# Graph attention layer with residual norm: first row tile's score products as three matmuls of 512 columns, with the off-diagonal part copied and added

## The reference

```python
u = einsum('bld,bmd->blm', h, h) / sqrt(384)
delta = softmax(u) * adjacency
attn = delta / (sum(delta, axis=2) + 1e-10)
# attn is split into above the diagonal, diagonal and below it
ctx = attn_left @ (h @ W_left.T + b_left) + diag_a * (h @ W_self.T + b_self) + attn_right @ (h @ W_right.T + b_right)
out = layernorm(x + relu(layernorm(ctx) * gamma + beta))
```

## Time and profile before

| what | value |
|---|---|
| median of 3 runs | 460.52 us (460.16 to 460.91) |
| profiled execution, its own time | 460.05 us |
| its span, first to last instruction | 458.3 us |
| PE busy | 448.5 us (98%), 2639 matmuls |
| DVE busy | 386.4 us (84%) |
| ACT busy | 322.1 us (70%) |
| POOL busy | 208.7 us (46%) |
| granted TensorE clock, mean | 0.994 of full speed |

### The profile page before, as it was taken

The page is one execution under the profiler, slowest core; times in us unless marked ns, Lnnn a source line. Parts: engine busy times, 40 slices in busy tenths (PEclk is TensorE's granted clock), DMA queues, the critical chain, the costliest instruction groups (busy, mean ns, idle before and its releaser), DMA issues.

```text
span 458.3 us, 9720 instructions
## 1 busy us (share of the span) xinstructions
PE 448.5 (98%) x2639; PEld 446.4 (97%) x2639; DVE 386.4 (84%) x1366; ACT 322.1 (70%) x710; POOL 208.7 (46%) x293
## 2 busy tenths in 40 slices
PE   8999999999999999999999999999999999999993
PEld 8999999999999999999999999999999999999992
DVE  5877988888898888988888988888889888987876
ACT  6756677677678677677677778677677677777753
POOL 0144346553345553345543445553345553344542
PEclk9999999999999999999999999999999999999997
DMA  8765455666456665555666555666445565554222
GB/s 259 224 207 176 136 173 184 197 197 196 137 179 194 188 195 177 169 175 183 189 195 186 157 178 183 188 208 193 150 163 191 182 200 182 159 176 155 92 69 93
DMA packets 84135, 80.60 MB, mean 176 GB/s; under 512 B 7058, under 2 KB 76436, under 8 KB 84116
## 3 DMA queue, kind: packets, MB, share of 16 engines
q1 hardware_dynamic: 84112, 80.38, 55.4%
q10 hardware_dynamic: 4, 0.00, 0.0%
HBM read 52.04 MB, written 28.31 MB: 175 GB/s over the span
## 4 chain that ended last, share of the span: by engine, by line
issue 29%; POOL 22%; DVE 15%; ACT 11%; PE 9%; DMA 8%; SPq 6%; POOLq 0%; DVEq 0%; ACTq 0%
POOL scaled L1111 7%; DMA dt_raw<-dt_dram 6%; POOL shifted L1115 6%; ACT normed L640 4%; SPq L319 4%; POOL rstd L1105 4%; ACT ps_scores L594 3%; DVE y_sb L876 3%; DVE proj_lo L832 3%; PE ps_proj L497 3%; POOL dt_right L1099 3%; DVE delta L801 3%; DVE cross_turned L768 2%; POOL dt_left L1099 2%; ACT dt_full L624 2%
## 5 line engine op out<-in xcount | busy, mean ns | idle before, releaser
L497 PE MATMUL ps_proj<-w_hi,xt_split 128*128 128x384 f32 x1128 | 236.4, 334 | 0.5 <-ACT ps_proj L610 0.5
L497 PEld LDWEIGHTS ps_proj<-w_hi,xt_split 128*128 128x128 f32 x1128 | 199.1, 188 | 0.8 <-ACT ps_proj L610 0.8
L497 PE MATMUL ps_proj<-w_lo,xt_split 128*128 128x384 f32 x564 | 128.0, 334 | 0.0
L1105 POOL TENSOR_TENSOR rstd<-var_eps,minus_half 128x4 f32<-128x4 f32 x31 | 34.7, 1119 | 184.2 <-DVE var_eps L862 184.2
L497 PEld LDWEIGHTS ps_proj<-w_lo,xt_split 128*128 128x128 f32 x564 | 100.5, 188 | 0.0
L610 ACT ACTIVATE ps_proj<-bias 128x384 f32<-128x384 f32 x188 | 90.5, 494 | 1.4 <-DMA bias<-in_L_gnn_b_self 0.7
L1111 POOL TENSOR_TENSOR scaled<-normed,gamma_sb 128x384 f32<-128x384 f32 x60 | 61.7, 1028 | 31.9 <-ACT normed L640 31.9
L614 ACT ACTIVATE proj_hi<-ps_proj 128x384 fp32r<-128x384 f32 x128 | 63.4, 496 | 13.0 <-PE ps_proj L497 12.6
L634 ACT ACTIVATE ps_ctx<-ps_proj,diag 128x384 f32<-128x384 f32 x64 | 35.5, 555 | 49.4 <-PE ps_proj L497 49.3
L832 DVE TENSOR_TENSOR proj_lo<-ps_proj,proj_hi 128x384 fp32r<-128x384 f32 x128 | 67.3, 544 | 1.8 <-ACT proj_hi L614 1.6
L1115 POOL TENSOR_TENSOR shifted<-scaled,beta_sb 128x384 f32<-128x384 f32 x61 | 62.5, 1024 | 2.5
(11 more groups left out here) (104 smaller groups left out, 675.3 us busy)
## 6 DMA issues: line engine op xcount, KB each, us to landing
x_sb<-in_x SPq DMA_DIRECT2D x32, 384.0 KB, 4.5
xt_sb<-in_x_t SPq DMA_DIRECT2D x31, 384.0 KB, 4.0
out_dram<-out_sb SPq DMA_DIRECT2D x31, 384.0 KB, 2.8
adj_sb<-in_adj SPq DMA_DIRECT2D x32, 256.0 KB, 4.5
dt_dram<-turned SPq DMA_DIRECT2D x31, 256.0 KB, 2.0
dt_raw<-dt_dram SPq DMA_DIRECT2D x124, 64.0 KB, 2.0
cross_dram<-cross_turned SPq DMA_DIRECT2D x29, 256.0 KB, 2.0
cross_raw<-cross_dram SPq DMA_DIRECT2D x116, 64.0 KB, 2.0
```

Of the source, the lines that this page charges most:

```text
L497: mm = nc.tensor.matmul(ps_proj[bank(at, g)][:, 0:H], halves[c][half], moving[w][:, c, :], start=False, stop=True, skip_group_check=True)
L1105: nc.gpsimd.tensor_tensor(rstd[at.slot(2)][:], var_eps[:], minus_half[:], ALU.pow).then_inc(rstd_ready, 1)
```

## The change

TensorE now makes the first row tile's scores with one matmul of 512 columns for each chunk, which leaves hi*hi and hi*lo off the diagonal in two groups (1 and 3). ScalarE copies group 1 to a new tile `cross_high`, and VectorE adds that to group 3 ahead of the turn. There are now four groups, so the whole bank is used, and the names of the groups move by one in the readers.

```diff
+        cross_high = sb("cross_high", [P, Q, R])
@@
         def blocks(t):
-            return ps_scores[:, t, 0:3 * P].rearrange("p (q k c) -> p q k c", q=Q, k=3)
+            return ps_scores[:, t, :].rearrange("p (q k c) -> p q k c", q=Q, k=4)
@@
         def exponentials(t):
-            return ps_scores[:, t, 0:3 * P].rearrange("p (q e) -> p q e", q=Q)[:, :, R:3 * R]
+            return ps_scores[:, t, :].rearrange("p (q e) -> p q e", q=Q)[:, :, 2 * R:4 * R]
+
+        def squares_of(tile):
+            first = tile[:, 0, 0:R]
+            return bass.AP(first.tensor, first.offset, [first.ap[0], [BANK + R, T], [4 * R, Q], [1, R]])
@@ cross
                 for c in range(C):
-                    nc.tensor.matmul(by_key(0, slice(0, 3, 2)), tile[:, c, 0:P], tile[:, c, 0:L],
-                                     start=(c == 0), stop=False, skip_group_check=True)
-                    nc.tensor.matmul(by_key(0, slice(1, 3)), tile[:, c, 0:P], tile[:, c, L:2 * L],
-                                     start=False, stop=(c == C - 1), skip_group_check=True)
+                    nc.tensor.matmul(by_key(0, slice(0, 4)), tile[:, c, 0:P], tile[:, c, :],
+                                     start=(c == 0), stop=(c == C - 1), skip_group_check=True)
                 for c in range(C):
-                    mm = nc.tensor.matmul(by_key(1, slice(0, 3)), tile[:, c, P:L], tile[:, c, P:2 * L],
+                    mm = nc.tensor.matmul(by_key(1, slice(1, 4)), tile[:, c, P:L], tile[:, c, P:2 * L],
@@ ScalarE
+            def copy_cross(at):
+                act.wait_ge(cross_ready, at.n(1, 1 - IN_FULL))
+                if at.b != IN_FULL:
+                    act.wait_ge(cross_added, at.n(1, -IN_FULL))
+                nc.scalar.activation(cross_high[:], blocks(0)[:, :, 1, :], ACT.Copy).then_inc(cross_copied, 1)
@@ ScalarE, one(at)
                     seed_proj(nxt, 1)
+                if ahead.exists(BATCHES):
+                    copy_cross(ahead)
                 if third.exists(BATCHES):
                     split_xt(third)
@@ VectorE
             def turn_cross(at):
                 dve.wait_ge(cross_ready, at.n(1, 1 - IN_FULL))
+                dve.wait_ge(cross_copied, at.n(1, 1 - IN_FULL))
+                other = blocks(0)[:, :, 3, :]
+                nc.vector.tensor_tensor(other, other, cross_high[:], ALU.add).then_inc(cross_added, 1)
+                dve.wait_ge(cross_added, at.n(1, 1 - IN_FULL))
+                nc.vector.memset(gate[:], 0.0)
                 if at.b != IN_FULL:
                     dve.wait_ge(cross_stored, at.n(16, -16 * IN_FULL))
@@ finish_scores
-                    square = ps_scores[:, :, 0:3 * P].rearrange("p t (q k c) -> p t q k c", q=Q, k=3)[:, :, :, 0, :]
-                    nc.vector.tensor_tensor(own, own, square, ALU.add).then_inc(own_added, 1)
+                    nc.vector.tensor_tensor(own, own, squares_of(ps_scores), ALU.add).then_inc(own_added, 1)
```

More of the change, by code:

```diff
@@ L220, in gnn_resnorm @@
         cross_ready = sem("cross_ready")
+        cross_copied = sem("cross_copied")
+        cross_added = sem("cross_added")
         own_added = sem("own_added")
@@ L419, in products @@
                         for i, j in pairs:
-                            mm = nc.tensor.matmul(by_key(t, slice(1, 3)), stationary[i], moving[j], start=clear,
+                            mm = nc.tensor.matmul(by_key(t, slice(2, 4)), stationary[i], moving[j], start=clear,
                                                   stop=(c == C - 1 and j == 0 and i == 1), skip_group_check=True)
@@ L768, in turn_cross @@
                 nc.vector.transpose(cross_turned[:].rearrange("p (q h t r) -> p t q h r", q=Q, t=T, r=R),
-                                    ps_scores[:, :, 0:3 * P].rearrange("p t (q k c) -> p t q k c", q=Q, k=3)[:, :, :, 1:3, :]
+                                    ps_scores[:].rearrange("p t (q k c) -> p t q k c", q=Q, k=4)[:, :, :, 2:4, :]
                                     ).then_inc(cross_turned_ready, 1)
@@ L800, in deltas @@
                         d, a = (tile[:, t, h * P:(h + 1) * P].rearrange("p (q c) -> p q c", q=Q) for tile in (delta, adj_sb[at.slot(UNROLL)]))
-                        nc.vector.scalar_tensor_tensor(d, blocks(t)[:, :, 1 + h, :], 1.0, a, ALU.mult, ALU.mult,
+                        nc.vector.scalar_tensor_tensor(d, blocks(t)[:, :, 2 + h, :], 1.0, a, ALU.mult, ALU.mult,
                                                        accum_out=sums[:, t, h:h + 1]).then_inc(delta_ready, 1)
```

## The result

The changed kernel takes 463.55 us in the median (461.70 to 464.42, 6 runs) against 460.48 (460.16 to 460.91, 6 runs): a ratio of 1.0063, with a 95% interval of 1.0043 to 1.0082. It is slower, by 3.1 us, and its six runs spread over 2.7 us where the six of before spread over 0.75. The execution that was profiled is the fastest of the six, 461.70 us with a span of 460.0, so its trace holds 1.65 us of the loss and not all of it: what made the other five slower stands in no trace of that comparison.

What follows compares the result with a forecast made beforehand. TensorE's stream bounds at 13.71 us a pass; the add makes the hidden VectorE-DMA loop 13.85, so 28 intervals cost 3.9, less 0.95 headroom: 2.9 more, 463.4 us. Range of 8 in 10: 459.6 to 466.8.

Steps and rivals of the forecast that it cites:

- The sum: Whole kernel: 28 intervals at 13.85 instead of 13.71 us give 3.9, less 0.95 of slack, so 2.9 us more.
- The bound moves from TensorE to the loop: Between the crosses: VectorE's round through the DMA queue becomes 13.85 us, above TensorE's 13.68, and takes over as the bound.
- the loop: Once a pass: transpose, store, dt_raw loads, ScalarE's split, VectorE's work to the next transpose; 13.50 us against TensorE's 13.71.
- the limit: At each cross: TensorE stalls once the exponentials start later than about 11.5 us after the cross.
- the signs: Trace from 34 to 418 us: about 3 us TensorE idle, crosses 13.8 to 13.9 apart, exponentials 11.5 after the cross.
- TensorE saves 0.03 us a cross: Cross matmuls: three of 512 columns replace six of 256, making TensorE's beat 13.68 us; at most 0.9 us in all.
- the first rival: VectorE's round stays hidden at 13.60 us, below 13.68; only TensorE's saving shows, 459.6 to 459.9 us; chance 0.36.
- The copy costs nothing, and nothing waits for it: ScalarE's 0.35 us copy fits into its existing waits; done at 228.14, before VectorE comes at 228.90, 0.76 us to spare.
- The add costs 0.35 us in the loop: VectorE ahead of the transpose: add, wait for its result and memset take 0.35 us, bounds 0.28 and 0.46.
- The round before was 13.50: Kernel before, transpose at 228.90 to the next at 242.40: 13.50 us, shortest seen 13.32, longest 13.92.
- the headroom: Slack before late exponentials stall TensorE at the cross: 0.55 us in a late pass, taken as 0.95 in the mean.
- late landings: DMA loads arriving late stretch one round to 13.92 us, 0.42 over 13.50.

Runs made afterwards that it cites:

- double add: The changed kernel with a second add of zeros, wait and memset behind the first, ahead of the transpose: 470.96 us, ratio 1.0228.
- the run with the copy alone: The kernel before plus ScalarE's copy of 128 x 128 to an unread tile and VectorE's wait for it, no add: 460.23 us against 460.30, ratio 1.0000.
- the matmuls alone: The changed kernel without ScalarE's copy and VectorE's add and waits, keeping the three 512-column matmuls: 460.40 us against 460.30, ratio 1.0008.
- the padded kernel: The changed kernel with always-met waits between the 512-column matmuls, making TensorE's program as long as with six of 256: 461.30 us, ratio 1.0024.
- the kernel with the add ahead: The kernel before, six matmuls of 256 columns, with an add of zeros, wait and memset ahead of the transpose: 461.01 us, ratio 1.0021.
- the kernel with room made: The changed kernel with two identity products moved into VectorE's wait for the exponentials and one statistics instruction behind the transpose: 461.71 us, ratio 1.0037.

## Why the prediction was right, and where its terms were not

The time was forecast at 463.4 and came to 463.55 first, then to 462.1 and 462.6 in two later sets of runs, against 460.3 of the kernel before. The direction and the mechanism hold; the near hit in the number is in part luck. The sum forecast 2.9 us more; the three comparisons gave 3.1, 1.9 and 2.2, and what parts the first from the later two stays open. And two errors in the sum cancel, as told below.

*The bound moves from TensorE to the loop.* Right. From the fifth cross on the exponentials sit at 11.43 to 11.9 us after the cross, 12.21 once (the limit was put at 11.5), and TensorE waits for `delta` at the cross. Of the signs, one was off: instead of about 3 us of idle time between 34 and 418 us TensorE shows 0.25 us less busy. The crosses from the fifth on are 13.78 apart in the mean, just under the forecast 13.8 to 13.9. The double add shows the loop's length passing into the time nearly one for one.

*TensorE saves 0.03 us a cross.* Wrong in size: 0.01 on the three that replace six, given back by the next three, beat 13.72 against 13.71. The fixed part of a 512-column matmul is not the 12 ns of the smaller ones: 0.70 / 3 = 233 ns is 20 ns above its 213. I had extrapolated from 118 and 173 ns; the first rival's gain of 0.6 to 0.9 us didn't exist at all. The fixed part of about 2.5 ns that I had taken from the Trainium skill (TensorE: Matmul & The Clock Gate, "Back-to-back issue gap") is further off still, though what I made of it (next to nothing saved) came out. That section gives it for the gap of isolated matmuls and not for a stream with a weight load for each, which this is.

*The copy costs nothing, and nothing waits for it.* Right, by the run with the copy alone, but for a wait of 0.9 us in the first of the 29 passes, while the exponentials are still far from their limit.

*The add costs 0.35 us in the loop.* Right: 0.32, and 0.42 in one pass of four, 0.34 in the mean; a second add lengthened the round by 0.33.

*The round before was 13.50.* This is the term that was off. The round with the add is 13.66, 13.66, 13.66 and 13.93 over the four passes of the unrolled loop, 13.73 in the mean, so that the part without the add was 13.39. I took an ordinary-looking pass of one trace for the mean where the shortest, 13.32, was the undisturbed one; the matmuls alone and the copy alone have 13.3 as their shortest too. Nor was 13.92 the longest: of the 28 rounds before, 8 are 14.18 to 14.36 us, and in 6 of these `rstd` is the slow one behind the split. In that kernel TensorE sets the mean of the rounds, so no mean of them gives the loop's own length. By my own sum, 28 x (13.73 - 13.71) less the headroom is no loss at all, and the add alone indeed costs only 0.7 us.

*What made up for it.* The sum knew late landings only as a spread of the round. They are the larger part: on one chip the copy and the add with six matmuls cost 0.5 of the changed kernel's 1.9 us, so 1.4 go with the form and where the transfers fall; on the other the padding took back 1.3 of 2.2. With a round within 0.02 us of the beat nothing is made up between them, so after the first 1.2 us the loop stays at its limit and every further one reaches TensorE. Before, such a landing also happened, ahead of the last cross, where VectorE waited 1.20 us for cross_raw and the cross was late by 0.07. That two of them come at bad moments in the changed kernel follows, as the padded kernel shows, from TensorE's shorter program, and is no part of my prediction.

*Not in it either:* the loop has two branches within some tenths of each other, one through the loads and one through VectorE's queue and GpSimd's `rstd`. I had followed the first.

## What to carry to other kernels

Before adding work to an engine with 14% of free time, measure the round of every loop that closes through it and take the undisturbed passes and the late ones apart: a loop 0.3 us under the bound looks idle, and it hides landings that come late. Taking three instructions out of a stream that is otherwise dense saves what start to start shows for the new size, and that has to be measured, not extrapolated. When two forms of one step differ by a per cent and all their waits look alike, compare where the instruction transfers fall in the DMA view.

## What the runs showed of the hardware

- The next matmul starts 233 ns behind one of 512 columns in this stream, where it is 118 behind 256 columns and 173 to 177 behind 384, at full granted clock.
- Instruction transfers of 16 KB on their own queue coincide with data loads that come late by 0.7 to 1.4 us (four loads issued in 3.09 us instead of 1.85, in 2.55 instead of 1.80, in 3.25 instead of 1.81). Not every late landing has one beside it: in the kernel with the add ahead VectorE waited 0.70 us at 320.12 for a load of cross_raw that landed 2.77 us after its issue, where the seven loads ahead of it took 1.96 to 2.05, and no instruction transfer stands in that trace between 124 and 414 us. The Trainium skill (Runtime: NRT & Kernel Launch, "Instruction fetch mechanics") says that an engine's instruction memory is refilled in blocks of 16 KiB and that the cost is mostly hidden. The size agrees with the 0.02 MB of the rows. That it is mostly hidden holds in the kernel before, whose last cross alone is 0.07 us late; in the changed one the padded kernel puts the place of the transfers at about 1.3 us. Through which resource the loads are held was not tried.
- The unrolled loop shows in the round: one pass of four takes 0.27 us longer, 0.1 of it between the add and the transpose (0.42 instead of 0.32). What it is was not tried.
- GpSimd's `rstd` of 128 x 4 elements lasts 1.02 us whenever it starts at least 8 ns ahead of VectorE's split of two SBUF inputs, even with the whole split beside it (the split then takes 0.73 us instead of 0.69 at most). When the split starts first or at most 3 ns behind, `rstd` ends 0.87 to 0.89 us after the split's end and lasts 1.40 to 1.57 us. This holds in all passes from 30 us on in the traces of all the kernels here. So work that arrives earlier on VectorE can make the whole round longer.
- The same order holds the other way round. In the kernel with room made, VectorE's product of 128 x 128 elements with two SBUF inputs lasts 0.28 to 0.29 us alone or when it starts 12 to 30 ns ahead of GpSimd's select of 128 x 256 (which then lasts 0.52 to 0.54 us instead of 0.42). Started behind the select it ends 0.14 us after the select's end, 0.48 in the mean over the trace; twice it started behind a GpSimd instruction of 128 x 384 that lasts 1.02 to 1.07 us, and lasted 1.08 and 1.10.
